# Layer 1's experts on blocks of 128 chosen rows instead of on all tokens

## The reference

```python
h = layernorm(x) * (1 + ca) + sa
x = x + ga * bias_attention(h)                     # 16 heads, a bias by distance
h = layernorm(x) * (1 + cb) + sb
h = h + mla(rmsnorm(h, g1))                        # causal, 16 heads
t = rmsnorm(h, g2).reshape(B * S, D)
logits = t @ gate_w                                # 8 experts
top_v, top_i = top_k(logits, 2)
gates = softmax(top_v)
combine = zeros((T, 8)).at[arange(T)[:, None], top_i].add(gates)
hid = silu(einsum('td,edh->teh', t, w1))           # w1: 8 x 128 x 256
ye = einsum('teh,ehd->ted', hid, w2)               # w2: 8 x 256 x 128
x = x + gb * (h + einsum('te,ted->td', combine, ye))
```

## Time and profile before

| | |
|---|---|
| median of 3 runs | 1983.15 us (1978.88 to 1984.26) |
| the profiled execution | 1975.98 us, its span 1974.0 us |
| busy in the span | PE 1731.3 us, DVE 1447.3, ACT 1000.0, POOL 586.7 |
| mean granted clock of PE | 0.951 |
| first shift of layer 1, first shift of slots 2, 6 and 9 | 701.8, 851.6, 1134.4 and 1360.4 us |
| last shift of layer 1 (step 1023) | 1885.0 us |

### The profile page before, as it was taken

How to read it: one execution, slowest core, us unless ns; L and a number is a source line. 1 busy time by engine, 2 the same in 40 slices (tenths; PEclk the granted TensorE clock), 3 DMA queues, 4 the chain that set the end, 5 groups by cost and what they waited for, 6 DMA issues and landing times.

```text
span 1974.0 us, 46459 instructions
## 1 busy us (share of the span) xinstructions
PE 1731.3 (88%) x17489; PEld 1157.3 (59%) x17489; DVE 1447.3 (73%) x4539; ACT 1000.0 (51%) x2018; POOL 586.7 (30%) x839
## 2 busy tenths in 40 slices
PE   3898898888958659989999999989999999988997
PEld 2677776776745436545655655655655555655455
DVE  6777877787651247887887887887887788787756
ACT  2554454545522236647646646646645645644642
POOL 3100111011114138635604613613623531530000
PEclk6999999999988779989999999999999999999999
DMA  4522122112008232122212213123122122121111
GB/s 120 179 74 61 34 66 79 57 39 63 8 10 276 58 99 72 53 78 80 75 59 90 67 56 107 50 73 101 43 72 79 62 76 76 69 68 61 50 33 50
DMA packets 109932, 144.30 MB, mean 73 GB/s; under 512 B 18752, under 2 KB 90880, under 8 KB 108432
## 3 DMA queue, kind: packets, MB, share of 16 engines
q1 hardware_dynamic: 76576, 113.28, 18.7%
q10 hardware_dynamic: 30128, 18.49, 3.3%
q0 software_dynamic: 3008, 9.57, 1.4%
HBM read 112.89 MB, written 28.15 MB: 71 GB/s over the span
## 4 chain that ended last, share of the span: by engine, by line
PE 51%; DVE 11%; issue 3%; ACT 2%; DMA 1%; SPq 1%; POOL 1%; ACTq 0%; DVEq 0%; POOLq 0%
PE ps L1955 10%; PE ps L1940 8%; PE ps L2096 5%; PE ps L2110 5%; PE ps L1994 5%; PE ps L2005 4%; PE ps L1965 3%; DVE ps L2184 2%; PE ps L1211 2%; PE ps L1220 1%; DVE l_XY L2184 1%; PE ps L2045 1%; PE ps L1967 1%; DVE l_xn L2222 1%; PE ps L2025 1%
## 5 line engine op out<-in xcount | busy, mean ns | idle before, releaser
L1759 POOL TENSOR_SCALAR l_XY<-l_XY,l_nmax 128x512 f32<-128x512 f32 x512 | 388.7, 768 | 224.6 <-DVE l_nmax L2184 216.4
L2184 DVE CUSTOM_DVE_ANT_0 l_XY<-ps,strips 128x512 f32<-128x512 f32 x512 | 341.1, 686 | 141.2 <-PE ps L1940 138.6
L1940 PE MATMUL ps<-l_stack 72*128 72x512 bf16 (+3 forms) x1024 | 351.1, 348 | 66.0 <-DVE l_nmax L2184 54.0
L1816 ACT ACTIVATE PT<-ps 128x512 f32<-128x512 f32 x512 | 305.3, 599 | 198.1 <-PE ps L1955 185.3
L1955 PE MATMUL ps<-ident,l_XY 128*128 128x128 f32 x2048 | 319.1, 279 | 3.7 <-POOL l_XY L1759 2.9
L1955 PEld LDWEIGHTS ps<-ident,l_XY 128*128 128x128 f32 x2048 | 240.5, 141 | 110.2 <-ACT PT L1816 45.1
L2184 DVE CUSTOM_DVE_ANT_0 ps<-ps,mask 128x384 f32<-128x384 f32 (+3 forms) x512 | 244.5, 504 | 27.0 <-PE ps L1940 24.6
L1940 PEld LDWEIGHTS ps<-l_stack 72*128 72x128 bf16 x1024 | 101.0, 99 | 148.2 <-DVE l_nmax L2184 84.3
L1965 PE MATMUL ps<-l_stack 75*128 75x256 bf16 (+3 forms) x512 | 155.2, 305 | 12.9 <-ACT PT_odd L1824 6.1
L1824 ACT ACTIVATE PT_even<-ps 128x512 f32<-128x512 f32 (+1 forms) x256 | 120.5, 493 | 63.6 <-PE ps L1967 51.8
L2096 PE MATMUL ps<-l_fT,l_w_e 128*128 128x512 f32 x256 | 145.1, 656 | 2.3 <-DVE h_tok L2383 1.2
...
## 6 DMA issues: line engine op xcount, KB each, us to landing
l_stack<-parts_dram SPq DMA_DIRECT2D x384, 96.0 KB
...
l_w_e<-in_L_ffn_w_dram ACTq DMA_DIRECT2D x128, 128.0 KB
...
w_e<-in_L_ffn_w_dram SPq DMA_DIRECT2D x12, 256.0 KB, 6.1
```

Of the source, the lines that this page charges most:

```text
L1759: nc.gpsimd.tensor_scalar(XY[:, c % XY_BUFS], XY[:, c % XY_BUFS], -1.0, nmax[:, c % 8:c % 8 + 1], ALU.mult, ALU.add).then_inc(y_pool, 1)
L1816: nc.scalar.activation(PT[:, quad(u, r), j], src.rearrange("p (k q) -> p k q", q=P), ACT.Exp).then_inc(moved, 1)
L1940: nc.tensor.matmul(ps[:, n % 3, 0:w], stack[0:STACK, 0, h, q * P:(q + 1) * P], stack[0:STACK, 1, h, 0:w], start=True, stop=True).then_inc( ...
L2184: nc.vector.tensor_tensor_reduce(out=dst, in0=src, in1=add, scale=-1.0, scalar=3.0e38, op0=ALU.add, op1=ALU.min, accum_out=low).then_inc(s ...
```

## The change

For batches 0 to 6 layer 1's experts are no longer computed for all tokens. Each token's row is put in DRAM once for each of its two experts, and the experts work on blocks of 128 rows:

- The batches are in three groups, `GROUPS = ((0, 1, 2), (3, 4), (5, 6))`. In a group each expert has a region of `rows_dram`, large enough for all its tokens. DVE counts for each token how many ahead of it in the group chose the same expert (`tally`, one product with a triangle of ones on PE, `place`), and POOL scatters the 512 normalised rows of the batch twice, with eight indirect DMAs of 128 rows (`scatter`, stage 21; `fold`, stage 8, adds gb * h to x on POOL).
- With the last batch of a group DVE writes a plan: for each block of 128 rows where it lies and which expert it belongs to (`plan_blocks`, five steps).
- The number of blocks is fixed: 16, 12 and 12 pairs of blocks for the three groups. The pairs run beside causal slots only, since their buffers lie in `XY`: four in slot 8, seven in slot 10, seven in slot 12 (the last two are the second group's), seven in slot 14, three in slot 15, one every six steps, and twelve from step 1038 on, one every three steps. DVE begins a bias slot only when all pairs so far are stored.
- For a pair, SP reads four numbers of the plan into registers and issues six DMAs with them (two blocks of rows, two experts' weights in three buffers), nine steps ahead, but not ahead of the output of the pair three before. PE transposes the rows, ACT copies, PE makes the hidden products of 128 columns in bank SIDE, tanh, product, the output in SIDE2, ACT copies, and SP stores the block.
- Later POOL gathers for each batch the two rows of each token with eight indirect DMAs, and DVE adds them with the gates (`gather_placed`, `add_placed`): batches 0, 1 and 2 from steps 0, 18 and 36 of slot 14, batches 3 and 4 from steps 26 and 46 of slot 15, batches 5 and 6 from steps 1070 and 1082. They share one buffer, so a gather waits for the addition ahead of it; the addition is 16 steps behind its gather.
- The rows of `rows_dram` are cleared by five DMAs of 2 MB.
- Batch 7 stays dense, as before.
- `QUADS` is 2 instead of 3, and `values` multiplies four tiles at once with 128 columns instead of eight with 256; the small buffers of batch 7's experts lie in `PT`.

The core of the diff:

```diff
@@ constants @@
-V_AT, W_AT = 13, 32
+V_AT, W_AT = 10, 32
-STAGES = dict(wo=1, add=3, square=4, power=5, scale=7, turn=10, logits=12, read=14, top0=15, top1=16, gap=18,
-              combine=20, first=12, each=6, second=2, tanh=1, mul=2, ye=9, half=2, sum=2)
+STAGES = dict(wo=1, add=3, square=4, power=5, scale=7, fold=8, turn=10, logits=12, read=14, top0=15, top1=16, count=18, gap=18,
+              gates=20, place=20, scatter=21, plan=22)
+GROUPS = ((0, 1, 2), (3, 4), (5, 6))
+REGION = [T * len(batches) for batches in GROUPS]
+PAIRS_OF = [(2 * T * len(batches) // P + E) // 2 for batches in GROUPS]
+PAIR_STAGES = dict(load=-9, turn=0, evac=1, hidden=3, tanh=4, mul=5, out=8, copy=9, store=10)
+PAIR_WINDOWS = ((0, TILES * PLACE[1, 3] + 36, 4, 6), (0, TILES * PLACE[1, 4] + 15, 7, 6), (0, TILES * PLACE[1, 5] + 15, 5, 6),
+                (1, TILES * PLACE[1, 5] + 45, 2, 6), (1, TILES * PLACE[1, 6] + 15, 7, 6), (1, TILES * PLACE[1, 7] + 3, 3, 6),
+                (2, MOE_START[B - 2] + 40, 12, 3))
+BLOCK_PAIRS = [(g, first + pitch * i) for g, first, count, pitch in PAIR_WINDOWS for i in range(count)]
+LOADS = {n: max(at + PAIR_STAGES["load"], MOE_START[GROUPS[g][-1]] + STAGES["plan"] + 6,
+                BLOCK_PAIRS[n - 3][1] + PAIR_STAGES["out"] + 1 if n >= 3 else 0) for n, (g, at) in enumerate(BLOCK_PAIRS)}
+CLEAR_AT = (40, TILES + 20, 3 * TILES + 50, 5 * TILES + 50)
+COMBINE_STAGES = dict(row=0, gather=0, add=16, done=17)
+COMBINE = {0: TILES * PLACE[1, 6], 1: TILES * PLACE[1, 6] + 18, 2: TILES * PLACE[1, 6] + 36,
+           3: TILES * PLACE[1, 7] + 26, 4: TILES * PLACE[1, 7] + 46,
+           5: MOE_START[B - 1] + 8, 6: MOE_START[B - 1] + 20}
-XY_BUFS, QUADS, W_BUFS, VW = 5, 3, 3, HD + 2
+XY_BUFS, QUADS, W_BUFS, VW = 5, 2, 3, HD + 2
@@ SP @@
+                def load_block_pair(n):
+                    ...
+                    if n >= 2:
+                        sp.wait_ge(block_x_turned, n - 1)
+                    if n >= W_BUFS:
+                        sp.wait_ge(block_y_ready, n - W_BUFS + 1)
+                    for k in range(2):
+                        j = 2 * i + k
+                        at = nc.values_load(plan[0:1, g % 2, 0, j:j + 1], engines=(mybir.EngineType.SP,), min_val=0, max_val=REGION_ROWS // P - 1)
+                        e = nc.values_load(plan[0:1, g % 2, 1, j:j + 1], engines=(mybir.EngineType.SP,), min_val=0, max_val=E - 1)
+                        sp.dma_start(x_b[:, n % 2, k, :], rows_dram[bass.ds(at, 1)].rearrange("a p c -> p (a c)")).then_inc(block_x_loaded[n % 2], 16)
+                        sp.dma_start(w1_b[:, n % W_BUFS, k, :], w1[bass.ds(e, 1)].rearrange("a p f -> p (a f)")).then_inc(block_w_loaded[n % W_BUFS], 16)
+                        sp.dma_start(w2_b[:, n % W_BUFS, k], w2[bass.ds(e, 1)].rearrange("a (f p) c -> p (a f) c", p=P)).then_inc(block_w_loaded[n % W_BUFS], 16)
@@ POOL @@
+                def scatter(b):
+                    g = GROUP_OF[b]
+                    pool.wait_ge(rows_chosen, b + 1)
+                    ...
+                    for k in range(2):
+                        for t in range(TT):
+                            nc.gpsimd.indirect_dma_start(rows_dram.rearrange("n p c -> (n p) c"),
+                                                         bass.IndirectOffsetOnAxis(ap=row_index[:, k, t:t + 1], axis=0),
+                                                         xf[:, t, :], None, bounds_check=REGION_ROWS - 1,
+                                                         oob_is_err=False).then_inc(rows_scattered[g % 2], 16)
+                def gather_placed(b):
+                    g, n = GROUP_OF[b], COMBINED.index(b)
+                    pool.wait_ge(planned, g + 1)
+                    wait_pairs_stored(pool, sum(PAIRS_OF[:g + 1]))
+                    if n:
+                        pool.wait_ge(x_done, X_DONE.index(COMBINED[n - 1]) + 1)
+                    ...
+                        if k == STAGES["fold"]:
+                            fold(b)
+                        if k == STAGES["scatter"]:
+                            scatter(b)
@@ PE @@
-                def values(u, r):
-                    ...
-                    first, second = quad(u, 0), quad(u, 1)
-                    pair = PT[:, first:second + 1] if second > first else PT[:, first::second - first]
-                    o = ps[:, o_bank(u // 2), u % 2 * 2 * P:(u % 2 + 1) * 2 * P].rearrange("p (r q) -> p r q", q=P)
-                    for k in (2 * r, 2 * r + 1):
+                def values(u, m):
+                    ...
+                    o = ps[:, o_bank(u // 4), q * P:(q + 1) * P]
+                    for k in range(TT):
@@ DVE @@
+                        if n % TILES == 0:
+                            wait_pairs_stored(dve, pairs_before(n))
+                    if k == p["top1"] + 1:
+                        tally(b)
+                    if k == p["place"]:
+                        place(b)
+                        gate_pair(b)
+                    if b == GROUPS[g][-1] and p["plan"] <= k < p["plan"] + 5:
+                        plan_blocks(g, k - p["plan"])
```

895 lines of the change are left out of this document (645 added, 250 removed).

## The result

The changed kernel takes 2127.0 us (median of 4 runs, 2117.7 to 2131.0) against 1981.6 for the kernel before on the same chip: a ratio of 1.072, 95% interval 1.070 to 1.074. The forecast was 2052, range 1985 to 2095. The direction was right; 75 us are missing. The profiled execution has a span of 2129.2 us against 1974.0, so the traces show 155 us to explain.

The account below looks back on a forecast made before the run. PE was taken as the bound (busy 88% of the span). Values +3, causal slots -13.4, slot 9 +2.5, SP's lag +3, slot 14 +12, slot 15 +9.7, tail +52: +68.8 us on 1976.0, 2052 at the median; range 1985 to 2095.

Parts of the forecast that it names:

- PE's work: Whole kernel: experts go and pairs come, so PE gives up 116 us; attention values in bias slots cost +3 us.
- I don't add it: Causal slots: a 9 us PE wait could lower the clock and cost some 2 us more each time; left out.
- the trace agrees: Clock 0.87 in slot 2's last part and 0.78 in slot 6's router part were said to fit the waits rule.
- Causal slots: Slots 4 and 6 take 64.1 us, -9.0 each; slot 8 -1.4; slots 10 and 12 +3.0 each; sum -13.4.
- The wait at `mx`: Causal slots: PE stands still 9.1 us at step 20, because eight scatter DMAs precede split_max on POOL.
- SP's lag behind stack loads, +3: Pair loads queued on SP behind attention's stack loads come late: +3 us over three slots, 0 to +10.
- Slot 9, +2.5: Slot 9's start: DVE waits for its first tile until pair 3 is stored, +2.5 us.
- Slot 14 (+12 for +25.9) and 15 (+9.7 for +32.6): Slot 14 +12 us, with power(1) some 5 us late; slot 15 +9.7, with two gathers ahead of split_max (+4, +5).
- The tail: Behind the last shift: nine pairs of 7.0 us each, end at T+141, 52 us longer (15 less or 31 more).
- R: Time of one plan read into a register on SP, four per pair: taken as 0.4 us.
- B: Rival: plan reads are dear (R near 1 us), SP also slower in slots 10, 12, 14: 2095; chance 0.15.
- C: Rival: PE's work decides and the wait at mx doesn't come: 1983, or 1968 with R low; chance 0.13.

Follow-up runs that it names:

- e1: Changed kernel with each batch's scatter one step later, behind split_max in POOL's queue: 2104.5 us, ratio 1.062 to the kernel before.
- e3: Changed kernel with 90 small PE products run in the first wait at mx of slots 4, 6, 8, 10, 12 and 14: 2124.4 us, ratio 1.070.
- e8: Kernel before, with the dense experts of batches 0 to 5 cut to 8 columns, same instructions, waits and loads: 1977.9 us, ratio 1.002.
- e10: As e8, with the hidden products of batches 0 to 5 back at 512 columns on PE alone: 1919.6 us, ratio 0.973.
- e6: As e5, with every score product of steps 0 to 23 of causal slots 4 to 14 run three times: 2061.2 us, ratio 1.041.
- e9: As e5, with the last twelve pairs five steps apart, last combinations later, and each gather's eight DMAs in eight steps: 2007.4 us, ratio 1.016.
- e5: As e1, with plan and tokens read before the weight-buffer wait and combinations moved behind power and split_max: 2057.5 us, ratio 1.039.
- e12: As e9, with pair loads 11 steps ahead, not 9, and seven wide constant products on PE in slots 4 to 12: 1992.8 us, ratio 1.009.
- e13: As e12, with the constant products also in slots 2 and 14 and up to step 31: 1990.8 us, ratio 1.011.

## Why the prediction was wrong, point by point

- **PE's work.** Right: 116 us less forecast, 122 less at full clock by the count above. The values in bias slots cost nothing (bias slots 485.1 us against 485.9), where +3 stood.
- **The step that failed: "I don't add it".** The clock was seen in the earlier trace rows (0.87 and 0.78), the rule that waits make what follows slower was weighed at 2 us a wait, and left out. In truth, by the count above, 117 us of PE's time went to it. The mechanism was mis-seen too: with the waits gone or filled most of the half-clock time stays (e1, e3), and the missing experts alone bring it (e8, e10). The prediction's "the trace agrees" was a misreading: in the two stretches that it names PE never waits for more than 1.9 us. The Trainium skill (TensorE: Matmul & The Clock Gate, "HAM oscillation — how this bites in real kernels") speaks of waits of PE; e8 has no new ones (none over 1.4 us in slot 6, at clock 0.64), and the measurement decides. The durations for causal slots came from slot 6's first parts (clock 1.00 and 0.78) and slot 2's last (0.87), and were taken as constants; in the changed kernel slots 4 to 12 ran at 0.66 to 0.79. What a us at half clock costs in a slot shows in slot 2, which has nearly the same work in all kernels: 46.0 us with 6.8 at half clock (e6), 47.5 with 10.2 (before), 52.9 with 23.9 (after): 0.40 us each.
- **Causal slots.** Slot 6 came as forecast, 64.4 for 64.1, but by two errors: the work at full clock would have given less, and 34 us at half clock, some 14 at 0.40 each, filled it. Slot 4 had 48 us at half clock and took 70.3. Slots 8, 10 and 12 are 8.4, 7.6 and 6.2 us over the forecast, at clock 0.78 and 0.79.
- **The wait at `mx`.** Right in place, cause and size (9.9 and 9.7 for 9.1). It wasn't worth its length: taking six of them away gained 22 us of 50.
- **SP's lag behind stack loads, +3.** Right in kind: in slot 8 a pair's load lay behind SP's wait for a landing (5.5 us in e1, 4.6 in e9), in the changed kernel 0.6 to 2.7 us.
- **Slot 9, +2.5.** It took 0.4 more.
- **Slot 14 (+12 for +25.9) and 15 (+9.7 for +32.6).** `power(1)` came late as said (PE waited 4.3 us). Not foreseen: the gather of batch 0 stops PE for 9.6 us (DVE and ScalarE for 10.4), and the later bursts cost too. e9's spread gathers took 23 us out of slot 14. In slot 15 the terms for the two gathers were right (4.5 and 6.9 us for 4 and 5), the clock (0.76) was not in the sum: 35 us more at half clock, some 14 us at 0.40 each. Two waits weren't in it either, 2.6 us for a pair's tokens and 3.8 for DVE.
- **The tail (+52 for +73.9).** The chain per pair was right: PE waits for the tokens ahead of each pair, 4.1 to 5.2 us for "some 5" (2.2 at the last). It was mis-sized: R is 0.66 and not 0.4, +1.1 us a pair; the output at half clock takes 2.05 us (1.05 at full clock, for the 1.1 of the sum) and waits 0.6, and the landing took 1.8 for 2.3. Nine pairs came 9.4 us apart in the mean (8.6 to 10.2) instead of 7.0: 22 us, all of the miss. From the last pair to the end it was 54 us for 56. The Trainium skill's floor of about 600 ns for a `tensor_load` (DMA: Bandwidth & Descriptors, "Latency and other measured facts"), which the prediction cites and leaves out of its sum, was nearer to the reads than its own 0.4.
- **The rivals.** B's cause (dear reads) was half true and gave 2095 only with R near 1. C's condition (no wait at `mx`) was made in e1, and the time was 2105 and not 1983. In e5 the later waits at `mx` are gone as well: 2058. What decided there instead was more than one thing: slot 4 of e1 is busy for 47.8 of 58.8 us at clock 0.74, and the stop at the gather stands in both. None of the four had the clock as its mechanism, nor the stop at the gathers.
- **A faster version.** None of the routed kernels was faster than the one before; the best are e12 and e13, at 1.009 and 1.011. Of the 152 us from slot 2 on, 19 to 21 were left. The tail alone is still 46 to 50 us longer than before.
- **Where the miss lies.** In the traces it is 155 less 69, 86 us: 28 in slots 4 to 12, 5 in slot 2, 14 in slot 14, 23 in slot 15, 22 in the tail and 4 ahead of layer 1, less 6 in the bias slots and the 3 for SP's lag. How much of each is the clock alone no run separates.
